# Score stack of an attention stage: heads side by side, filled in two halves by four transfers each

## The reference

```
src_trans = (ctx @ W_src.T + b_src) * mask      # keys, values: 256 + 256 channels
tgt_trans = (layernorm(x) @ W_tgt.T + b_tgt) * mask   # queries: 256 channels
k, v, q  -> 8 heads of 32 channels
scores = q.k / sqrt(32);  -inf where mask == 0;  attn = softmax(scores)
x = x + tanh(g) * (concat([layernorm(x), attn.v]) @ W_out.T + b_out)
```

## Time and profile before

| | |
|---|---|
| median of 3 runs | 686.91 us (684.88 to 689.09) |
| the profiled execution | 686.24 us, of which 684.2 us from its first to its last instruction (the span) |
| busy shares of the span | PE 94%, DVE 63%, ACT 62%, POOL 29% |
| granted TensorE clock, mean | 0.995 of 2.4 GHz |
| waits of PE for mask transfers / for shift rows | 5.6 us in 10 / 7.6 us in 5 |
| DMA | 58.01 MB, mean 85 GB/s |

### The profile page before, as it was taken

One profiled execution on the slowest core, in us unless ns is written; L12 is line 12 of the kernel. 1 busy time (PEld: TensorE's weight loads), 2 busy tenths in 40 slices (PEclk: granted clock), 3 DMA queues, 4 the chain that ended last, 5 costly groups with the idle time before them and its releaser, 6 DMA issues.

```text
span 684.2 us, 10968 instructions
## 1 busy us (share of the span) xinstructions
PE 643.1 (94%) x3497; PEld 439.2 (64%) x3497; DVE 430.1 (63%) x982; ACT 425.4 (62%) x1149; POOL 201.3 (29%) x299
## 2 busy tenths in 40 slices
PE   5988899999999998699999999999999987899997
PEld 3754555555543357588878777887887865556654
DVE  7973847776776648477667666666566686152522
ACT  7766655535544433587777778777777777545452
POOL 6574424210110012133444332323332220242110
PEclk9999999999999999999999999999999999999999
DMA  8821116501000005543433554434345440001112
GB/s 276 246 98 62 62 32 260 85 1 62 0 1 1 0 0 127 127 94 99 117 94 99 126 125 99 116 99 113 100 100 126 94 95 2 1 17 45 56 38 92
DMA packets 43130, 58.01 MB, mean 85 GB/s; under 512 B 13152, under 2 KB 24002, under 8 KB 42818
## 3 DMA queue, kind: packets, MB, share of 16 engines
q1 hardware_dynamic: 43074, 57.33, 30.9%
HBM read 27.46 MB, written 4.19 MB: 46 GB/s over the span
## 4 chain that ended last, share of the span: by engine, by line
PE 64%; SPq 15%; DMA 6%; DVE 4%; POOL 4%; issue 3%; ACT 3%; DVEq 0%; POOLq 0%; ACTq 0%
SPq L513 13%; PE bank L1147 12%; PE bank L1159 6%; DMA c_stack<-neg_row 5%; PE bank L1567 4%; PE bank L1362 4%; PE bank L1432 4%; PE bank L1371 4%; PE bank L1385 3%; PE bank L1408 3%; PE bank L1344 3%; PE bank L1557 3%; PE bank L1123 3%; SPq L528 2%; PE bank L1558 2%
## 5 line engine op out<-in xcount | busy, mean ns | idle before, releaser
L936 ACT ACTIVATE c_junk<-bank,c_nmx 128x256 bf16<-128x256 f32 x256 | 117.2, 484 | 15.5 <-DVE c_nmx L1894 15.3
L1894 DVE TENSOR_REDUCE c_nmx<-bank 128x4 f32<-128x1024 f32 x64 | 75.3, 1218 | 38.5 <-PE bank L1385 38.5
L1147 PE MATMUL bank<-b_o,cw 128*128 128x512 f32 x192 | 90.6, 603 | 1.8 <-ACT b_o L804 1.8
L780 ACT ACTIVATE b_h<-bank,cb 128x512 f32<-128x512 f32 x48 | 32.8, 686 | 51.0 <-PE bank L1147 51.0
L958 ACT ACTIVATE c_pT<-bank 128x1024 f32<-128x1024 f32 x64 | 61.6, 1013 | 4.3 <-PE bank L1408 4.3
L1046 ACT ACTIVATE d_h<-bank,b_col 128x512 f32<-128x512 f32 x64 | 39.6, 686 | 39.4 <-PE bank L1558 39.4
L1147 PEld LDWEIGHTS bank<-b_o,cw 128*128 128x128 f32 x192 | 34.5, 190 | 44.9 <-issue 41.1
L1344 PE MATMUL bank<-c_ctxT,wsrcT 128*128 128x256 f32 x256 | 61.5, 385 | 0.4 <-DVE c_vb L1886 0.4
L1362 PE MATMUL bank<-wsrcT,c_ctxT 128*128 128x256 f32 x240 | 56.7, 379 | 0.0
L936 ACT ACTIVATION_READ_ACCUMULATOR c_junk<-bank,c_nmx 128x1 f32 x256 | 55.6, 217 | 0.0
L1408 PE MATMUL bank<-c_stack 99*128 99x256 f32 x256 | 46.9, 313 | 7.8 <-DMA c_stack<-c_rows 7.6
(11 more groups left out here) (190 smaller groups left out, 1289.3 us busy)
## 6 DMA issues: line engine op xcount, KB each, us to landing
c_stack<-c_parts SPq DMA_DIRECT2D x192, 128.0 KB
a_ctx<-in_ctx SPq DMA_DIRECT2D x16, 512.0 KB, 4.0
c_ctxT<-turned_ctx SPq DMA_DIRECT2D x16, 512.0 KB, 4.3
out_x<-x_sb SPq DMA_DIRECT2D x7, 512.0 KB, 2.9
x_sb<-in_x SPq DMA_DIRECT2D x3, 1024.0 KB, 11.2
mask_b<-in_mask_BxS_fk SPq DMA_DIRECT2D x1, 2048.0 KB, 11.6
x_sb<-in_x SPq DMA_DIRECT2D x2, 512.0 KB, 5.4
wsrcT<-turned_w_src SPq DMA_DIRECT2D x1, 1024.0 KB, 5.8
```

Of the source, the lines that this page charges most:

```text
L936: op = nc.scalar.activation(c_junk[:, tc, j, :], scores(tc)[:, j, :], ACT.Exp, bias=c_nmx[hg][:, tc, j:j + 1], accum_out=c_sum[hg][:, tc, ...
L1147: op = mm(bank[2 * u + h][:], cw1[:, c, h * P:(h + 1) * P], b_o[n % LANES][:, c, :], start=c == 0, stop=c == DK - 1)
L1894: v.tensor_reduce(c_nmx[hg][:, tc, :], scores(tc), AXIS.X, ALU.max, negate=True)\
```

## The change

The channels of K and Q within a head group are put in another order, on the host, by permuting the rows of W_src's key part, of W_tgt and of both biases: partition p of a head group now holds channel p // 4 of head p % 4, so that the heads lie side by side. `c_parts` is laid out by head group first, then part (Q_LO, K_HI, Q_HI, K_LO), so that a part pair is a run of 2 KB. The stack is laid out by head group, head, side.

One transfer then takes a part (128 KB) or a pair of neighbouring parts (256 KB) of a head group from all 128 partitions to the 32 rows of a third, for four heads. A head group has four transfers: K_HI and Q_HI for the first third, the pair Q_LO, K_HI for the second, Q_HI, K_LO for the third; 1.5 MB for a batch as before, in pieces of 1 KB or 2 KB.

Each head group has a semaphore of its own; the mask, for both groups, counts on the first. `scores_c` of head group 0 waits for the first alone, that of head group 1 for both; POOL's splits wait for both. SP's order becomes: rows of the batch before, first half, mask, rows of this batch (hg 0), second half, context. The wait of `stack_c` for transposed scores goes by head group, and the mask waits for those of the whole batch that the stack held.

```diff
-Q_LO, Q_HI, K_HI, K_LO = range(PARTS)
+Q_LO, K_HI, Q_HI, K_LO = range(PARTS)
-STACK_DMAS = 3 * QH + 1
+STACK_DMAS = (4 + 1, 4)
...
-c_stack[0] = sb("c_stack0", [MASK_ROW + 1 + SHIFTS, 2, QH, DK, S], F32R, st)
+c_stack[0] = sb("c_stack0", [MASK_ROW + 1 + SHIFTS, DK, QH, 2, S], F32R, st)
-c_parts = sb("c_parts", [P, PARTS, DK, S], F32R, st)
+c_parts = sb("c_parts", [P, DK, PARTS, S], F32R, st)
...
-def stack_c(b, s, thirds):
+def stack_c(b, s, hg):
...
-    need(sp, c_sT_ps, 2 * TS * (b - 1))
+    need(sp, c_sT_ps, TS * (2 * (b - 2) + hg + 1))
...
-    for c in thirds:
-        first, step = ((Q_HI, K_HI - Q_HI), (Q_LO, K_HI - Q_LO), (Q_HI, K_LO - Q_HI))[c]
-        for j in range(QH):
-            sp.dma_start(
-                c_stack[s][c * HD:(c + 1) * HD, :, j, :, :].rearrange("p a g t -> p a (g t)").bitcast(F32),
-                c_parts[j * HD:(j + 1) * HD, first:first + step + 1:step, :, :]
-                .rearrange("p a g t -> p a (g t)").bitcast(F32)).then_inc(c_stack_in, 16)
+    for c, a, part, count in ((0, 1, K_HI, 1), (0, 0, Q_HI, 1), (1, 0, Q_LO, 2), (2, 0, Q_HI, 2)):
+        sp.dma_start(
+            c_stack[s][c * HD:(c + 1) * HD, hg, :, a:a + count, :].rearrange("p j a t -> p j (a t)").bitcast(F32),
+            c_parts[:, hg, part:part + count, :].rearrange("p a t -> p (a t)").bitcast(F32))\
+            .then_inc(c_stack_in[hg], 16)
...
 def masks_c(b, s):
+    need(sp, c_sT_ps, 2 * TS * (b - 1))
...
-stack_c(0, 0, range(3))
+stack_c(0, 0, 0)
 masks_c(0, 0)
+stack_c(0, 0, 1)
...
     if b + 1 < B:
-        stack_c(b + 1, 1 - b % 2, (0, 1))
+        stack_c(b + 1, 1 - b % 2, 0)
+        masks_c(b + 1, 1 - b % 2)
     rows_c(b, b % 2, 0)
     if b + 1 < B:
-        stack_c(b + 1, 1 - b % 2, (2,))
-        masks_c(b + 1, 1 - b % 2)
+        stack_c(b + 1, 1 - b % 2, 1)
...
 def split_k(b):          # split_q(b) likewise
-    need_alone(pool, c_stack_in, 16 * STACK_DMAS * b, s_passed)
-    nc.gpsimd.tensor_copy(c_parts[:, K_HI, :, :], c_kT[:]).then_inc(c_k_split, 1)
+    for hg in range(2):
+        need(pool, c_stack_in[hg], 16 * STACK_DMAS[hg] * b)
+    nc.gpsimd.tensor_copy(c_parts[:, :, K_HI, :], c_kT[:]).then_inc(c_k_split, 1)
...
 def scores_c(b, s, hg):
-    need(pe, c_stack_in, 16 * STACK_DMAS * (b + 1))
+    need(pe, c_stack_in[0], 16 * STACK_DMAS[0] * (b + 1))
+    if hg == 1:
+        need(pe, c_stack_in[1], 16 * STACK_DMAS[1] * (b + 1))
...
+def heads_side_by_side(a):
+    a = np.asarray(a)
+    return np.swapaxes(a.reshape((DK, QH, HD) + a.shape[1:]), 1, 2).reshape(a.shape)
```

More of the change, by code:

```diff
@@ L174, in build @@
           w_src, b_src, w_tgt, b_tgt, w_out, b_out, u1, v1, b1, u2, v2, b2,
-          ctx_turned, w_src_turned, w_tgt_turned, w_out_turned, out):
+          ctx_turned, w_src_turned, w_tgt_turned, w_out_turned, b_k_column, b_q_column, out):
     x_dram = x.rearrange("b (k p) d -> b p k d", p=P)
@@ L384, in build @@
             "kT_in_psum", "kT_ready", "qT_in_psum", "qT_ready", "v_in_psum", "v_biased", "v_ready"))
-        c_k_split, c_qhi_ok, c_qlo_ok, c_stack_in = (sem("c_" + n) for n in (
-            "k_parts_ready", "q_high_ready", "q_low_ready", "stacks_in"))
+        c_k_split, c_qhi_ok, c_qlo_ok = (sem("c_" + n) for n in ("k_parts_ready", "q_high_ready", "q_low_ready"))
+        c_stack_in = [sem(f"c_stacks{hg}_in") for hg in range(2)]
         c_s_ps, c_mx_ok, c_sum_ok, c_ln_ok, c_inv_ok = (sem("c_" + n) for n in (
@@ L693, in split_q @@
                 need_alone(pool, c_q_ok, b + 1, s_passed)
-                need_alone(pool, c_stack_in, 16 * STACK_DMAS * b, s_passed)
-                nc.gpsimd.tensor_copy(c_parts[:, Q_HI, :, :], c_qT[:]).then_inc(c_qhi_ok, 1)
+                for hg in range(2):
+                    need(pool, c_stack_in[hg], 16 * STACK_DMAS[hg] * b)
+                nc.gpsimd.tensor_copy(c_parts[:, :, Q_HI, :], c_qT[:]).then_inc(c_qhi_ok, 1)
                 need(pool, c_qhi_ok, b + 1)
-                nc.gpsimd.tensor_tensor(c_parts[:, Q_LO, :, :], c_qT[:], c_parts[:, Q_HI, :, :].bitcast(F32),
+                nc.gpsimd.tensor_tensor(c_parts[:, :, Q_LO, :], c_qT[:], c_parts[:, :, Q_HI, :].bitcast(F32),
                                         ALU.subtract).then_inc(c_qlo_ok, 1)
@@ L1384, in scores_c @@
                     for j in range(QH):
-                        op = mm(scores(tc)[:, j, :], c_stack[s][0:MASK_ROW + 1, 0, j, hg, tc * P:(tc + 1) * P],
-                                c_stack[s][0:MASK_ROW + 1, 1, j, hg, :], start=True, stop=True)
+                        op = mm(scores(tc)[:, j, :], c_stack[s][0:MASK_ROW + 1, hg, j, 0, tc * P:(tc + 1) * P],
+                                c_stack[s][0:MASK_ROW + 1, hg, j, 1, :], start=True, stop=True)
                     op.then_inc(c_s_ps, 1)
@@ L1407, in scoresT_c @@
                 for j in range(QH):
-                    op = mm(scores(q)[:, j, :], c_stack[s][rows, 1, j, hg, q * P:(q + 1) * P],
-                            c_stack[s][rows, 0, j, hg, :], start=True, stop=True)
+                    op = mm(scores(q)[:, j, :], c_stack[s][rows, hg, j, 1, q * P:(q + 1) * P],
+                            c_stack[s][rows, hg, j, 0, :], start=True, stop=True)
                 op.then_inc(c_sT_ps, 1)
@@ L2054, in features_first, with columns @@
         return np.ascontiguousarray(np.swapaxes(a, -3, -2))
+    def heads_side_by_side(a):
+        a = np.asarray(a)
+        return np.swapaxes(a.reshape((DK, QH, HD) + a.shape[1:]), 1, 2).reshape(a.shape)
+    def columns(a):
+        return np.ascontiguousarray(heads_side_by_side(a).reshape(DK, P).T)
+    w_src, b_src = np.asarray(inputs["L1_xattn_W_src"]), np.asarray(inputs["L1_xattn_b_src"])
     return {"turned_ctx": features_first(inputs["ctx_2048"], FK),
-            "turned_w_src": features_first(inputs["L1_xattn_W_src"], FK),
-            "turned_w_tgt": features_first(inputs["L1_xattn_W_tgt"], DK),
-            "turned_w_out": features_first(inputs["L1_xattn_W_out"], 2 * DK)}
+            "turned_w_src": features_first(np.concatenate([heads_side_by_side(w_src[:D]), w_src[D:]]), FK),
+            "turned_w_tgt": features_first(heads_side_by_side(inputs["L1_xattn_W_tgt"]), DK),
+            "turned_w_out": features_first(inputs["L1_xattn_W_out"], 2 * DK),
+            "column_b_k": columns(b_src[:D]), "column_b_q": columns(inputs["L1_xattn_b_tgt"])}
 def kernel(**inputs):
```

16 lines of the change are left out of this document (8 added, 8 removed).

## The result

The changed kernel takes 702.19 us (median of 4 runs, 697.45 to 702.9), the kernel before 686.69 beside it: a ratio of 1.0194, interval 1.0157 to 1.0231. The forecast was 678.9. The profiled execution took 702.22 us against 686.24, 16.0 us more.

The account below looks back on a forecast made before the run. TensorE, busy 643.1 of 684.2 us, was taken as the bound, so gains come from idle time: 5.6 (mask waits) + 0.5 (row waits) + 1.6 (start) - 0.4 (semaphores) = 7.3 us, 686.24 to 678.9 us; range 674.0 to 683.5.

Parts of the forecast that it names:

- I reckon with 3.5: Stack transfers: a half of 768 KB takes 3.5 us at the old burst rate of 221 GB/s; 2.0 was the alternative.
- the sum had 2.53: Start of the stage: 2.53 us from the rows' issue to TensorE's start, so transposed scores at 281.3 instead of 284.60.
- the rows queueing behind the wide half: Slower rival: rows leave SP too late behind the half, from 1.14 us per issue on; 700 us, chance 0.07.
- the 21 us: Slower rival: at 1.49 us from issue to issue each of 15 batches loses 1.4 us, 21 us more.
- drains at well under half its rate: Slower rival's second way: a half, partly in 1 KB pieces, drains so slowly that rows are equally late; within the 0.07.
- Mask waits: Score products (L1385): ten waits for the mask transfer, 5.6 us over the run, were to go.
- SP's issue: SP's queue: 0.64 us from issue to issue whatever the bytes or pieces; first half leaves from 434.55 to 437.1.
- Rows issued at once: Steady batches: SP is free by 437.9, so rows go out within 0.3 us of ACT's copy.
- The extra semaphore waits on TensorE and POOL: Added cost: one more wait per batch on TensorE, 0.4 us taken (bounds 0 and 0.8); POOL's four per batch hidden.
- the 1.6 us of new gain: Start of the stage: SP begins batch 1's stack at 274.6, rows leave 3.3 us earlier; 1.6 us beyond the mask wait.
- The clock: TensorE's clock after the start's wait: 3.1 us of idling remain, so nothing given back; bounds 0 and 1.7 us.
- a rival of its own at 677.2: Rival: TensorE's clock stays up at the start of the stage, 1.7 us more gain; 677.2 us, chance 0.20.

Follow-up runs that it names:

- e3: The kernel before with only its mask transfer moved ahead of the rows, after the first eight stack transfers, old shapes kept: 694.51 us, ratio 1.0115.
- rows by three: The changed kernel with the 32 channels of a row range written to every third row of the stack: 676.74 us, ratio 0.9863 to the kernel before.
- e1: The changed kernel with each pair transfer split in two single parts, six transfers of 128 KB for each half: 692.35 us, ratio 1.0052.

## Why the prediction was wrong

**The step that failed** is "I reckon with 3.5" us for a half, in the paragraph on the transfers. It put the price between the rates of the two transfers that the trace held, 32 partitions to 32 and a load to 128, and had no end below them, though a transfer wide at one end only was in neither. It measured 5.5 us at 145 GB/s, and so the rows behind it landed 4.44 us after their issue, where the sum had 2.53. Nothing in the trace excluded a loss there; a bound as far below the old rate as the load stood above it (221 x 221 / 385 = 127 GB/s) would have held the result, with 6 us for a half; that it comes out at the 127 measured later is chance.

The paragraph leaned on the Trainium skill ("SBUF — State Buffer", Door 1: The DMA port swizzle): 32 rows reach half of the ports. That sorts what was measured into two groups rightly: by it partitions 0 to 63 reach no more ports than 0 to 31 (131 beside 127), and a range across both halves reaches all (258, and 377 for every fourth row). But read as the prediction read it, a narrow destination also holds the old rate, whatever the source, and that is what failed: 127 instead of 218. Measurement decides; the count of ports gave an upper bound here.

**The rival that came true** was the right one by its title, the rows queueing behind the wide half, but that its 700 us are near the 702.19 is luck: the 21 us were worked out for slow issues on SP, which stayed at 0.6 us. Its other branch, a half that "drains at well under half its rate", set the point too far out. The half drains at two thirds of its rate (145 of 221), and that was enough: with the 2.53 us of before, rows issued at 452.85 would have landed by 455.4, TensorE needs them at 456.84 (457.29 - 0.45), and so 1.5 us were all the slack there was. Kernel e3 shows that there was hardly any in the kernel before. With 0.07 the chance was too low for a step without a row.

**Right, step by step.** Mask waits: 5.6 us forecast to go, 5.1 went. SP's issue: 2.52 us for four, as taken. Rows issued at once: 0.04 us behind ACT. The extra semaphore waits on TensorE and POOL: 0.4 us was taken, too little to tell apart here.

**Wrong as a consequence.** *The start:* the 1.6 us of new gain became a loss, since SP's start was taken from DVE's chain, moved up by 1.45 us, and not from when the transfers have read c_parts, on which POOL waits (15.25 us until 274.47). *The clock:* forecast to fall as before, it cost 6.0 us more, at the start, at 414.5 and around 600. At 414.5 POOL's split of v_sb, which stands ahead of its split of Q there, may have helped to make the half late; that was not tried alone.

**With the failed step mended** the rest holds: rows by three, with the change's order, issues and semaphores, took 678.61 us in its profiled execution against the forecast of 678.9. Two errors are in that agreement. The clock stayed up at the start (1.00 from 281 to 295, where it was 0.88), which was a rival of its own at 677.2; and the start was 0.8 us later than forecast, mostly because the stage itself began some 0.65 us later in this execution (DVE's K bias at 268.21 instead of 267.56). The median, 676.74, is 2.2 us under the forecast.

**What stays open:** why rows within one half of the partitions take 126 to 135 GB/s from a spread source and 218 to 238 from neighbours. How a transfer's pieces are dealt to the 16 engines might explain it; no view shows that. Why the rows landed earlier in e1, with its singles at nearly the same drain, is open too, and so are 2.5 us of TensorE's extra busy time.

## What to carry to other kernels

Here fewer, wider transfers were cheaper on the issuing queue alone; before merging, price the drain as well, and where the trace has no transfer of that shape, keep an end of the range below every rate it shows. What is issued behind a slow transfer landed late here from SP's queue and from ACT's, so ask which small, urgent transfer comes next. Where the order of rows is free, as in a sum over partitions, try them spread over both halves of the partitions: here one slice made 25 us.

## What the runs showed of the hardware that was not expected

A copy inside SBUF from 128 partitions to 32 rows ran at 127 GB/s with the rows side by side, 129 on every second, 231 on every third, 377 on every fourth. From every fourth partition to 32 rows side by side it was 126 as well, so reading few partitions doesn't help. The first 0.2 MB or so of a burst are taken up much faster than the rest drains (336 GB/s in the half microsecond from 32.0, 115 from 32.5), so a short burst alone hides the slow rate. After a wait of 3.19 us the clock stayed at 2.4 GHz (rows by three), after one of 2.80 us (414.78 in the changed kernel) it was at 1.2: the length of one wait did not decide it. Small operations of DVE, 0.17 us each, lasted 0.52 to 1.18 us beside POOL's splits and ended 0.02 to 0.03 us after an operation of POOL (changed kernel, 275.7 to 279.6).
